# Gram matrices of 2048 batches: the first tile of a lap turned whole, four-lane stores in more groups, and two loads held back at the start

## The reference

```
r_inputs: 2048 x 64 x 256, float32
Z = einsum("bnd,bmd->bnm", inputs, inputs)        # 2048 Gram matrices, 64 x 64
li, lj = tril_indices(64, k=-1)
return Z[:, li, lj]                                # 2048 x 2016, float32
```

## Time and profile before

| what | value |
|---|---|
| median of 3 runs | 398.48 us (398.1 to 398.72) |
| the profiled execution | 397.29 us |
| its span, from the first to the last instruction | 395.5 us |
| TensorE busy with matmuls | 368.8 us, 93% of the span |
| VectorE busy | 370.4 us, 94% |
| ScalarE busy | 188.3 us, 48% |
| moved by DMA | 150.99 MB, 382 GB/s over the span |
| read from HBM, written to it | 134.22 MB, 16.52 MB |

### The profile page before, as it was taken

The page is one execution under the profiler, slowest core; times in us unless marked ns, Lnnn a source line. Parts: engine busy times, 40 slices in busy tenths (PEclk is TensorE's granted clock), DMA queues, the critical chain, the costliest instruction groups (busy, mean ns, idle before and its releaser), DMA issues.

```text
span 395.5 us, 69567 instructions
## 1 busy us (share of the span) xinstructions
PE 368.8 (93%) x33280; PEld 363.7 (92%) x33280; DVE 370.4 (94%) x369; ACT 188.3 (48%) x858; POOL 200.3 (51%) x975
## 2 busy tenths in 40 slices
PE   4389999999999999999999999999999999999960
PEld 4389999999999999999999999999999999999960
DVE  3258899999999999999999999999999999999995
ACT  0021245454545555555555455545554555545572
POOL 2000075482828456382837557282846648282765
PEclk9569999999999999999999999999999999999995
DMA  8999999999999999999999999999999999994307
GB/s 321 423 421 419 423 422 418 380 424 423 416 405 389 427 420 423 398 422 418 411 422 362 426 423 422 416 419 421 413 420 377 427 414 417 385 416 162 114 16 193
DMA packets 21274, 150.99 MB, mean 382 GB/s; under 512 B 2688, under 2 KB 2816, under 8 KB 4864
## 3 DMA queue, kind: packets, MB, share of 16 engines
q1 hardware_dynamic: 18912, 136.81, 85.5%
q10 hardware_dynamic: 2336, 13.94, 8.7%
HBM read 134.22 MB, written 16.52 MB: 381 GB/s over the span
## 4 chain that ended last, share of the span: by engine, by line
DVE 44%; issue 29%; PE 24%; ACT 0%; DVEq 0%; ACTq 0%
DVE x_turned L232 31%; PE bank_set L309 24%; DVE row_halves L249 11%; DVE x_in L256 1%; DVE packed_rows L154 1%; DVE packed_rows L143 0%; ACT packed_rows L143 0%; DVE x_turned L261 0%; DVEq L248 0%; ACT products L336 0%; DVEq L75 0%; DVEq L279 0%; ACTq L332 0%
## 5 line engine op out<-in xcount | busy, mean ns | idle before, releaser
L309 PE MATMUL bank_set<-x_turned 32*64 32x64 f32 x33280 | 368.8, 237 | 13.1 <-issue 11.1
L309 PEld LDWEIGHTS bank_set<-x_turned 32*64 32x64 f32 x33280 | 363.7, 131 | 18.0 <-issue 11.7
L232 DVE STREAM_TRANSPOSE x_turned<-x_in 128x1024 f32<-128x1024 f32 x256 | 295.7, 1207 | 19.3 <-PE bank_set L309 15.6
L154 POOL COPY packed_rows<-row_halves 32x32 f32<-32x32 f32 (+30 forms) x930 | 191.7, 206 | 187.5 <-DVE row_halves L249 149.9
L336 ACT COPY products<-bank_set 128x512 f32<-128x512 f32 x128 | 75.1, 586 | 146.6 <-PE bank_set L309 130.9
L249 DVE STREAM_TRANSPOSE row_halves<-products 128x1024 f32<-128x1024 f32 x60 | 72.2, 1203 | 0.0
L143 ACT COPY packed_rows<-row_halves 128x32 f32<-128x32 f32 (+30 forms) x465 | 61.2, 218 | 12.5 <-DVE row_halves L249 12.3
L149 ACT COPY packed_rows<-row_halves 128x128 f32<-128x128 f32 x240 | 54.1, 300 | 15.0 <-DVE row_halves L249 13.3
L336 ACT ACT_TABLE_LOAD x1 | 1.3, 1283 | 26.0 <-PE bank_set L309 26.0
L154 POOL COPY packed_rows<-x_in 32x32 f32<-32x32 f32 (+30 forms) x31 | 5.0, 212 | 2.2 <-DVE x_in L256 2.2
L256 DVE STREAM_TRANSPOSE x_in<-products 128x512 f32<-128x512 f32 (+1 forms) x5 | 4.6, 995 | 0.0
## 6 DMA issues: line engine op xcount, KB each, us to landing
x_in<-x_dram SPq DMA_DIRECT2D x128, 1024.0 KB, 15.1
y_dram<-packed_rows ACTq DMA_DIRECT2D x20, 504.0 KB, 8.9
y_dram<-packed_rows SPq DMA_DIRECT2D x4, 504.0 KB, 5.0
y_dram<-packed_rows ACTq DMA_DIRECT2D x6, 252.0 KB
y_dram<-packed_rows ACTq DMA_DIRECT2D x24, 63.0 KB
y_dram<-packed_rows SPq DMA_DIRECT2D x1, 380.0 KB
y_dram<-packed_rows ACTq DMA_DIRECT2D x1, 380.0 KB
y_dram<-packed_rows SPq DMA_DIRECT2D x1, 124.0 KB
```

What stands on the lines that cost most here:

```text
L154: return copy(packed_rows[first:first + BLOCK, group % 2, :, at + BLOCK:at + i], halves(group)[first + BLOCK:first + HALF, i, :, 0:i - BLOCK])
L232: nc.vector.transpose(x_turned[:, j, chunks].rearrange("p c b s (h u n v) -> p u v (c b s h) n", h=ROWS // BLOCK, u=PAIRS, v=PAIR), x_in[: ...
L309: done = nc.tensor.matmul(bank_sets[j][side * HALF:(side + 1) * HALF, g, slot, :].rearrange("r (n u v) -> r u n v", u=PAIRS, v=PAIR), rows ...
```

## The change

The number of parts in which a tile is turned and multiplied now depends on its place in the lap: one part at place 0, two halves at place 1. The two blank tiles' zeros are written as before, and they count for both parts or for the one. The stores go by few in every group up to 12 whose number is no multiple of four: 1, 2, 3, 5, 6, 7, 9, 10 and 11. The loads of tiles 3 and 4, the fourth and the fifth, wait now: the fourth until tile 0 is turned, the fifth until the first half of tile 1 is turned. All later loads come behind them on SyncE.

```diff
+    HELD = (3, 4)
     LAP = 2
+    PARTIALS = (1, 2)
-    PARTIALS = 2
-    PARTIAL = CHUNKS // PARTIALS
...
-        turned = [[semaphore(f"turned{j}_{h}") for h in range(PARTIALS)] for j in range(LAP)]
+        turned = [[semaphore(f"turned{j}_{h}") for h in range(PARTIALS[j])] for j in range(LAP)]
...
+        def chunks_of(j, h):
+            some = CHUNKS // PARTIALS[j]
+            return range(h * some, (h + 1) * some)
...
         def by_few(group):
-            return group % 2 == 1 and group <= FEW_UNTIL
+            return group % 4 != 0 and group <= FEW_UNTIL
...
                 if t >= IN_RING:
                     lap, j = place(t - IN_RING)
-                    sync.wait_ge(turned[j][PARTIALS - 1], (lap + 1) * LAP)
+                    sync.wait_ge(turned[j][-1], (lap + 1) * LAP)
+                elif t in HELD:
+                    lap, j = place(t - HELD[0])
+                    sync.wait_ge(turned[j][0], (lap + 1) * LAP)
                 sync.dma_start(x_in[:, k], x_joined[t * PARTS:(t + 1) * PARTS]).then_inc(loaded[k], 16)
...
-                for h in range(PARTIALS):
-                    chunks = slice(h * PARTIAL, (h + 1) * PARTIAL)
+                for h in range(PARTIALS[j]):
+                    chunks = slice(chunks_of(j, h).start, chunks_of(j, h).stop)
                     dve.wait_ge(multiplied[j][h], lap)
...
             def multiply(j):
-                for h in range(PARTIALS):
+                for h in range(PARTIALS[j]):
                     pe.wait_ge(turned[j][h], count)
                     for slot in range(SLOTS):
-                        last_slot = h == PARTIALS - 1 and slot == SLOTS - 1
+                        last_slot = h == PARTIALS[j] - 1 and slot == SLOTS - 1
...
-                        for c in range(h * PARTIAL, (h + 1) * PARTIAL):
+                        for c in chunks_of(j, h):
```

More of the change, by code:

```diff
@@ L98, in gram_lower_triangle @@
         loaded = [semaphore(f"loaded{k}") for k in range(IN_RING)]
-        turned = [[semaphore(f"turned{j}_{h}") for h in range(PARTIALS)] for j in range(LAP)]
+        turned = [[semaphore(f"turned{j}_{h}") for h in range(PARTIALS[j])] for j in range(LAP)]
         kept = [semaphore(f"set_kept{s}") for s in range(SETS)]
-        multiplied = [[semaphore(f"multiplied{j}_{h}") for h in range(PARTIALS)] for j in range(LAP)]
+        multiplied = [[semaphore(f"multiplied{j}_{h}") for h in range(PARTIALS[j])] for j in range(LAP)]
         rows_turned = semaphore("rows_turned")
@@ L203, in _ @@
             for j in range(BLANK):
-                nc.gpsimd.memset(x_turned[:, j, PARTIAL:CHUNKS], 0.0).then_inc(turned[j][1], LAP)
+                nc.gpsimd.memset(x_turned[:, j, CHUNKS // 2:CHUNKS], 0.0).then_inc(turned[j][-1], LAP * PARTIALS[j] // 2)
             for group in range(GROUPS):
@@ L260, in _ @@
             for j in range(BLANK):
-                nc.vector.memset(x_turned[:, j, 0:PARTIAL], 0.0).then_inc(turned[j][0], LAP)
+                nc.vector.memset(x_turned[:, j, 0:CHUNKS // 2], 0.0).then_inc(turned[j][0], LAP * PARTIALS[j] // 2)
             turned_rows = 0
@@ L331, in keep @@
                 group, in_group = divmod(t, GROUP_TILES)
-                act.wait_ge(multiplied[s][PARTIALS - 1], lap + 1)
+                act.wait_ge(multiplied[s][-1], lap + 1)
                 if group >= KEPT_RING and in_group == 0:
```

## The result

| | before | changed |
|---|---|---|
| median of 6 runs each | 398.19 us | 401.24 us (400.78 to 401.58) |
| the profiled execution, its span | 397.29, 395.5 us | 401.27, 399.2 us |

The change makes the kernel slower: the ratio is 1.0076, 95% interval 1.0063 to 1.0089, or 3.05 us. The two profiled executions are 3.98 us apart.

The account below looks back on a forecast made before the run. VectorE was taken to set the pace, with loads hidden by 3.3 us at tile 120. A 4.4 us load delay, waiting away 6.0 us of compute gain, gave 401.7, or 402.9 us by the median; range 392.5 to 406.

Parts of the forecast that it names:

- four late engines: Four DMA engines carrying all 4-lane stores: they end loads at 369 us, and the change makes them 9.0 us later.
- gain of the computation: Compute path of TensorE and VectorE: 6.0 us gained, 4.2 at the start and 1.8 over the laps, all waited away.
- The sum: Four engines 9.0 us later, 5.8 spare at tile 120, so 3.2 late there; 1.2 more at group 12's store: 4.4.
- 4 of 16: Sign in the windows after the last load's issue: DMA share about 4 of 16 engines, not 5.
- slow engine: A fifth late engine, last to land at 371.5 us, pays 4.3 us per whole store; the new groups save it 3.6.
- The starved start: Held loads leave the DMA engines dry at the start: +2.9 us on all later loads, bounds 0 and +5.2.
- The three groups: Small stores newly in groups 2, 6 and 10: 2.0 us a group, +6.1 us on the four engines, bounds 5.5 and 9.7.
- account of the four: The four engines' time from 2.9 to 369 us less 128 loads leaves 47 us for stores: 24.0 thousand bytes per us.
- an idle DMA makes the later stops shorter: TensorE's second and third stops at the start shrink; steady work begins near 17 instead of 21.28 us, -4.2 us.
- The lap: VectorE's two-tile lap falls from 5.63 to 5.57 us, so TensorE's 5.60 bounds it: -1.8 us over 59 laps.
- rival 1: Lateness of the DMA engines doesn't bind and the compute path shows its 6.0 us gain: 392.5 us; chance 0.24.
- A's sums: Follow-up expectations from the theory that small stores and starved start delay a few DMA engines, costing only beyond their spare time.

Follow-up runs that it names:

- e4: The changed kernel with each small store of 4 lanes made 16 lanes by a quarter of the columns: 402.55 us, ratio 1.0118.
- e5: The kernel before with the whole first tile of a lap alone; no held loads, small stores in the odd groups: 397.22 us, ratio 0.9982.
- e3: The changed kernel without the two held loads; whole first tile and small stores in nine groups stay: 400.45 us, ratio 1.0082.
- e12: The changed kernel with small stores in the odd groups only and shorter holds of the fourth and fifth load: 394.18 us, ratio 0.9920.
- e11: The changed kernel with one side stored by 7, 7, 7, 7, 4 lanes in five groups, fifth load held until tile 1 is turned: 420.37 us.
- e1: The kernel before with small stores in nine groups instead of six and nothing else changed: 399.67 us, ratio 1.0046.
- e6: The kernel before with the two held loads alone; small stores in the odd groups, all tiles by halves: 396.26 us, ratio 0.9954.
- e2: The changed kernel with small stores in the odd groups only; held loads and whole first tile stay: 395.20 us, ratio 0.9940.
- seven-lane runs: Three runs of the changed kernel with small stores of up to 7 lanes, in nine or five groups: 412.74, 414.05 and 420.37 us.

## Why the prediction was right

**The place and the mechanism held.** The prediction put the price on four late engines, which 4-lane stores make later, and said that the gain of the computation would be waited away. VectorE does wait for x_in in the last third, landing passed 25 us, and e4 shows the four engines appear and vanish with the shape of the stores. The rule quoted from "DMA: Bandwidth & Descriptors" (the Trainium skill, section "Why a DMA increments its semaphore by 16 and not by 1") agrees with e4's share of one engine and the change's share of five.

**The sum held where it was made.** The prediction has the four finish tile 120 at 351.6 + 9.0 = 360.6, 3.2 us late for the computation. In the change this load is issued at 330.1 and lands 30.5 us later, at 360.6. The delay that stays comes from tile 118, in front of which VectorE waits last: it lands at 355.7 and is turned at 355.81, where tile 118 was turned at 351.77 before, one lap ahead of tile 120's 357.40. So the delay is 4.0 us, 4.4 were forecast. Tile 127 is 3.8 later.

**Five engines, not four, were late at the end, and this doesn't speak against the sum.** The sign "4 of 16" didn't follow from the prediction's own terms: the slow engine, 3.6 us sooner by the new groups and 2.9 later by the start, would end at 371.5 - 0.7 = 370.8, and the windows from 362 to 368 lie before that. The 16 parts of tile 127's load, the last, land so:

| run | eleven by | the other five |
|---|---|---|
| before | 357.8 | 365.1, 368.3, 368.7, 369.5, 371.4 |
| e5 | 356.7 | 364.9, 368.2, 369.4, 369.8, 370.9 |
| e3 | 359.6 | 368.8, 371.1, 374.4, 375.4, 377.1 |
| the change | 361.0 | 371.0, 373.8, 377.4, 377.9, 378.4 |

In the change the earliest of the five takes 9.4 us from tile 120 to tile 122, 4.5 more than two loads, with the whole store of group 12 between. Before, it was the last of the five that paid so much for that store (9.2 us from tile 118 to tile 120). So the earliest should be the slow engine, 0.4 us sooner than before, and the other four are 8.7 to 9.2 us later, where the sum had 9.0. The trace doesn't name the engines; that the parts are matched rightly is inferred from this price.

**Its terms were off, and one fitted by luck.** The starved start was put at 2.9 us, and 4.1 was measured. The step that is wrong there takes tile 3's lateness for that of all loads: tile 4 waits for half of tile 1 and comes another 1.2 us later. Yet by the last load only 1.3 to 3.0 us of it are left (the last four parts of e3 and of the change), so 2.9 came near the end by luck. The three groups were put at 6.1 us, and the last four parts of e3 are 6.0 to 7.3 us later than the first four of e5. Two sums are out by little: the account of the four begins at 0.7 + 4.9 - 2.49 = 3.1 and not 2.9, and load 3 is 17.4 - 14.6 = 2.8 later.

The computation's gain was put at 6.0 us; e12, where nothing waits, shows tile 127 3.1 us earlier than before. There the start brings 2.2 and not 4.2, because the third stop didn't shrink. That an idle DMA makes the later stops shorter was wrong for the third: e11 leaves one load in flight there, and it is 4.06 us all the same. The lap came as forecast. Since all this gain was waited away, its error didn't reach the forecast, but rival 1's 392.5 was too low by 1.7 against e12.

**The median.** 402.9 us was made by adding 1.19 us, by which the profiled execution before lies under its median of three. The profiled execution after lies on its median (401.27 and 401.24). So 1.2 of the 1.7 us between forecast and result come from there.

**What stays open.** A's sums for single parts were off by 0.4 us in e1, 1.2 in e3, 2.8 in e6 and 4.3 in e2. Most of all, held loads with six groups end up 1.3 to 2.1 us late at tile 120 where they began 4.1 late. The late engines must have spent 2 to 3 us less on the same stores or loads; no run here separates that. What sets the length of a stop of TensorE isn't shown either. The seven-lane runs don't say which of the engines is the slow one, only that 4 lanes don't use it and 7 lanes do.

## What to carry to other kernels

A DMA share near 1 over 16 engines can hide a few engines that fall further behind with each store, and a load is there only when the last of them has finished: follow the landing time through the run, and read the share after the last issue, which counts the late ones. An edit that costs little while there is spare time costs its full price once another edit has used that up, so parts that were tuned one by one have to be timed together. Holding back early loads to let a program's own fetches through pays as long as the loads are given back in time; release them at the earliest event that serves the purpose.

## What the runs showed of the hardware

TensorE's stops at the start end when a block of its program has come in. After each of the first two it goes on with 127 or 128 matmuls and as many weight loads. Each stop has one packet of 0.02 MB on an instruction queue, q8, which moves four in the whole run. These are the queue's lines for 12.9 to 14.0 us in the kernel before and for 10.2 to 11.6 us in the change; the last figure is the packet's time as a share of 16 engines, which makes 1.0 and 1.4 us:

```profile
q8 instruction: 1, 0.02, 5.8%
...
q8 instruction: 1, 0.02, 6.1%
```

The packet starts at 12.94 us before, 1.4 us after the second stop begins, and at 10.21 in the change, 1.1 us ahead of it. In both TensorE goes on 1.2 to 1.3 us after the packet is through. So the second stop is short in the runs with held loads (1.2 to 1.9 us, 3.68 before) where its block was on the way ahead of it. "Runtime: NRT & Kernel Launch" in the Trainium skill, section "Instruction fetch mechanics", says that each engine's sequencer fetches its program in blocks of 256 instructions through a DMA queue of its own; 128 matmuls with 128 weight loads agree with that.

The number of loads in flight doesn't by itself set how long a stop is. The first is 3.64 us with eleven loads issued and 3.50 with three. The third is 4.05 us in the change, with loads 3 to 10 in flight, and 4.06 in e11 with load 3 alone.

One of the 16 DMA engines is slower than the others at stores. By the landing times it paid 4.3 us for a whole group, where the four's own account gives 64.5 / 24.0 = 2.7 (both are the prediction's estimates), and in e4 its part of tile 120 lands 20.6 us after the other fifteen. "DMA: Bandwidth & Descriptors" in the Trainium skill, section "Latency and other measured facts", names engines 7 and 15 as usually slower, and ties this, as a guess, to the descriptor rings of DMAs that GpSimd issues. The stores here are issued by ScalarE and SyncE. By the rule of the lowest-numbered engines that the prediction quotes from that page, the one here would be one of 4 to 6, which 7 lanes use and 4 don't; no run here shows which.

TensorE's clock fell in the middle of a run when it had to wait. In e4 it stood still for 2.36 us, and the granted clock in the windows that follow goes from 0.91 to 0.50 (1.2 GHz) and 0.73, with 157 matmuls in 2 us in place of about 200:

```profile
358.72 7.49 PE L318 MATMUL bank_set<-x_turned 32*64 32x64 f32 x578 [2.36 <-DVE x_turned L241]
...
358.00:360.00 2.00, 1.28 (x113) 1.28 (x116) 2.00 (x3) 0.17 (x2) 1.68 (x9) 0.91 0.48 201
360.00:362.00 2.00, 2.00 (x157) 2.00 (x148) 2.00 (x2) 0.93 (x8) 1.31 (x7) 0.50 0.08 29
362.00:364.00 2.00, 2.00 (x181) 2.00 (x170) 1.42 (x2) 1.42 (x8) 0.00 (x0) 0.73 0.08 33
```

The next whole tile then waits 0.58 us for TensorE. A late load can so cost more than its own wait.
